# Decays' exponentials on ScalarE, tables spread two per transfer, and query and key products right behind a norm group's turns

## The chip, the cores and the metric

The kernel runs on one core of a Trainium2 chip. The metric is the device time in microseconds (us), the median of the runs.

## What is computed

The reference is a two-layer tower over 16 sequences of 129 tokens with 512 features. A tokenizer makes the tokens; then come a gated-scan layer, a mixture of experts, gated linear attention (GLA), and a second mixture of experts, each with a layer norm ahead and a residual. The change touches the tokenizer and the first pass of the attention.

```python
# tokenizer: 128 heads, 64 states, 512 positions, 16 batches
P = dt_Lambda[..., None] * t - P_max[..., None]
S = jnp.exp(P)                                     # complex
Wc = Wc * num * recip
K = jnp.einsum('chn,hnl->chl', Wc, S).real
...
# attention
q = x @ Wq.T
k_sig = jax.nn.sigmoid(x @ Wk.T)
q = jax.nn.silu(q) * SCALE
gf = jax.nn.log_sigmoid(-k_sig)
o = _gla(q, k_sig, x, gf)
go = o @ Wog.T + x @ Wig.T
```

## The kernel before, in words

**Programs and queues.** Each engine (SyncE for DMAs, VectorE, GpSimd, ScalarE, TensorE) runs one program, written out in order: tokenizer, scan layer, experts, attention, experts. There is no planner. An engine does its instructions in program order, and semaphores hold it where it needs another's result.

**Tokenizer.** Position l is split as 64a + 8b + c, with a, b and c from 0 to 7, so exp(P) is a product of three small tables (`NG` = 3 groups of `TB` = 8 values). The 128 partitions hold 64 states for heads 0 to 63 (`LO`) and the same states for heads 64 to 127 (`HI`). VectorE computes the step sizes, the decay exponents `ke` (L251, 128x1536), the sine and cosine arguments (`im`, `re`), multiplies them by the exponentials (L304), negates one (`ni2`, L306), then forms the coefficients and from them `car`, `ncai`, `ncar` (L338 to L344). ScalarE takes the exponential of `ke` (L392) and the sines (L395, L396). `tab` holds six tables for all 128 heads on both halves; SyncE fills it by SBUF-to-SBUF DMAs of 64 KB (`spread`, L163): for each of four blocks of 32 heads eight for the decay tables (`tables`) and four for the factors (`factors`), 48 in all. The first block's `tables` go when `tabr` is 1, its `factors` when `tabr` is 2, that is behind L344.

The main loop has eight chunks of 16 heads. ScalarE copies the chunk's factors to PSUM (L405), VectorE builds U in two halves (L355, L362, L363), GpSimd builds B (L384, L386, L388), TensorE multiplies them (L429, one product for each head, each in two passes in the trace's count, so x32 is a chunk), ScalarE copies the product out (L416), and SyncE stores it to DRAM (L185) and loads it back with heads on partitions (L192, L215). The scan layer's norm (L482) starts when the last load has landed.

**Attention's first pass.** There are 17 token tiles; the class-token tile (16 rows) goes first, i = 0, and tile n has i = n + 1. VectorE norms them in groups i = 0, 1 to 4, 5 to 10 and 11 to 16 (L482, L506, Newton steps L516 to L522, then one L527 for each tile). TensorE turns each normed tile by four transposes (`turn_tile`, L538) into one of three PSUM banks, ScalarE copies it out (L1946), and TensorE multiplies four copied tiles at a time by the query and key weights (`project`, L2027, eight passes of 512 columns). ScalarE takes query and key out of each product (`band_of`, L1958 and L1959). In TensorE's order `project(-1)`, of the class tokens, stands behind turn 3, `project(0)` behind turn 6, `project(1)` behind turn 10, `project(2)` behind turn 14, and `project(3)` behind turn 16. In ScalarE's order `band_of(0)`, (1) and (2) stand behind the copies of turns 7, 11 and 15, `band_of(3)` at the end. Turn i waits until the copy of turn i-3 is done; `project(q)` waits for the copy of turn 4q+4. Behind the bands come two sigmoids over all sequences (L1974, L1975), a scan and a reciprocal on VectorE (L1816, L1818), and the second pass on TensorE (`xw_of` and `gate_x`, L2055), which begins with turns of its own.

Of the kernel before, what the change touches and what calls it, by code (L numbers as in the profile page):

```python
# [11 lines left out]
ALU = mybir.AluOpType  # L12
# [90 lines left out]
def tokenizer(nc, sem, sb, ps, d, h0, hb, h_in, t_in, stored):  # L103
# [21 lines left out]
    m, kl, ke, mk, re, im = (a.take(NG, HH, TB) for _ in range(6))  # L125
    ni2, car, ncar, ncai, ta, tb = (a.take(HH, TB) for _ in range(6))
    tab = a.take(6, NH, TB)
    R1, I1, D1, D2, A1, A2 = range(6)
# [30 lines left out]
    def sync(sp):  # L159
        def spread(to, half, src, frm, k, s):  # L160

            cols = slice(2 * HC * (k % 2), 2 * HC * (k % 2) + 2 * HC)
            sp.dma_start(tab[half, to, 2 * HC * k:2 * HC * (k + 1), :], src[frm, cols, :]).then_inc(s, 16)  # L163

        def tables(k):
            frm = LO if k < 2 else HI
            for to, lo, hi in ((R1, re[:, 0], re[:, 0]), (D1, re[:, 1], im[:, 1]), (I1, im[:, 0], im[:, 0]), (D2, ni2, re[:, 1])):
                spread(to, LO, lo, frm, k, t_in[k])
                spread(to, HI, hi, frm, k, t_in[k])

        def factors(k):
            frm = LO if k < 2 else HI
            for to, lo, hi in ((A1, car, ncai), (A2, ncai, ncar)):
                spread(to, LO, lo, frm, k, t_in[k])
                spread(to, HI, hi, frm, k, t_in[k])
# [21 lines left out]
        sp.wait_ge(t_in[0], 8 * 16)  # L197
        factors(0)
        for k in range(1, 3):
            tables(k)  # L200
            factors(k)
# [15 lines left out]
    def vector(v):  # L217
# [27 lines left out]
        c.link(v.scalar_tensor_tensor(out=ktf, in0=kc[:, 1, 0:NK], scalar=pos[:, 0:1], in1=kc[:, 0, 0:NK], op0=ALU.mult, op1=ALU.add))  # L245
# [5 lines left out]
        v.tensor_tensor(ke, k24, along(dre), ALU.mult).then_inc(ker, 1)  # L251

# [29 lines left out]

        c.put(v.tensor_tensor(m, k24, along(fhi), ALU.mult))
# [58 lines left out]
        c.put(v.tensor_tensor(car, ta, tb, ALU.subtract))  # L342
        c.link(v.scalar_tensor_tensor(out=ncai, in0=ncai, scalar=-1.0, in1=ncar, op0=ALU.mult, op1=ALU.subtract))
        v.tensor_tensor(ncar, tb, ta, ALU.subtract).then_inc(tabr, 1)  # L344
        v.wait_ge(w_in, 64)
# [19 lines left out]
    def gpsimd(g):  # L365
        for k in range(NHC):
            u = k % 2
            hh = slice(k * HC, (k + 1) * HC)
            if u == 0:
                if k == 0:  # L370
                    g.wait_ge(tabr, 2)
                g.wait_ge(t_in[k // 2], 12 * 16 if k else 8 * 16)
# [17 lines left out]
    def scalar(s):  # L390
        s.wait_ge(ker, 1)
        s.activation(ke, ke, ACT.Exp).then_inc(sines, 1)  # L392
# [5 lines left out]
        def factors(k):  # L398

            if k % 2 == 0:  # L400
                s.wait_ge(t_in[k // 2], 12 * 16)
# [1941 lines left out]
```

## Time and profile before

| | |
|---|---|
| median of 3 runs | 1573.73 us (1570.84 to 1576.62) |
| profiled execution | 1577.39 us, its span 1575.6 us |
| mean granted TensorE clock | 0.968 of full speed |

```profile
PE 1390.4 (88%) x6461; PEld 1080.0 (69%) x6462; DVE 838.1 (53%) x1729; ACT 373.3 (24%) x711; POOL 480.1 (30%) x350
```

This line gives busy time, share of the span and instructions of each engine: PE is TensorE's matmuls, PEld its weight loads, DVE VectorE, ACT ScalarE, POOL GpSimd; SPq is SyncE's queue of DMAs. A tile is named by its tensor: `sb` is the tokenizer's working memory, `ps` PSUM, `moe_xn` the normed tiles, `moe_scratch` holds the turned tiles, `tokens` and `h_rows` are DRAM. The chain that ended last is followed back from the last instruction of the program; its lengths run from one step to the next. In the busy lists, "x8" is a run of eight instructions, and the bracket tells the idle time ahead of it and what ended it.

### The profile page before, as it was taken

Reading aid. Unit: us, or ns where it says so; the run is one execution under the profiler, and the core shown is the slowest. Engines: PE = TensorE matmul, PEld = TensorE weight load, DVE = VectorE, ACT = ScalarE, POOL = GpSimd, SP = SyncE. Lnnn points to the kernel's source line nnn. Section 1 sums busy time; section 2 is a strip of 40 time slices with the busy share of each in tenths; the row PEclk is TensorE's granted clock in tenths of the full one; section 3 lists DMA queues with packets and bytes.
Section 4 is the critical chain, followed back from the end, with each engine's and each line's share of the span. In section 5 each row is a group of like instructions: output and inputs, shape, how many; then the busy total and the mean of one; then the engine's idle time right before and its main releaser. Section 6 shows DMA issues by size and latency. Waiting matters only on the chain.

```text
span 1575.6 us, 21975 instructions
## 1 busy us (share of the span) xinstructions
PE 1390.4 (88%) x6461; PEld 1080.0 (69%) x6462; DVE 838.1 (53%) x1729; ACT 373.3 (24%) x711; POOL 480.1 (30%) x350
## 2 busy tenths in 40 slices
PE   0595648999999999379999889999999999999997
PEld 0583316888544444237777578888888889999896
DVE  8875597755322222563667775555555543333332
ACT  1113113111111111242222312232333212222221
POOL 0661430252244443100111015632332203343332
PEclk9999779999999999798999999999999999999999
DMA  4493005201865554700000403656666579776443
GB/s 97 89 161 39 0 21 179 104 21 63 304 149 93 87 89 72 204 22 0 1 0 1 182 21 97 206 199 212 208 221 225 189 267 361 243 198 185 78 73 41
DMA packets 88931, 197.16 MB, mean 125 GB/s; under 512 B 28657, under 2 KB 32753, under 8 KB 85361
## 3 DMA queue, kind: packets, MB, share of 16 engines
q1 hardware_dynamic: 68768, 154.33, 30.1%
q0 software_dynamic: 20096, 42.02, 14.6%
q8 instruction: 33, 0.54, 0.1%
q14 instruction: 34, 0.27, 0.1%
HBM read 112.24 MB, written 81.02 MB: 123 GB/s over the span
## 4 chain that ended last, share of the span: by engine, by line
PE 79%; DVE 13%; issue 3%; DMA 2%; ACT 1%; POOLq 1%; POOL 0%; SPq 0%; DVEq 0%; ACTq 0%
PE ps L1533 25%; PE ps L1593 19%; PE ps L1655 9%; PE ps L2055 6%; PE ps L1681 4%; PE ps L429 4%; PE ps L1623 2%; DVE held L482 2%; PE ps L538 2%; PE ps L1669 1%; PE ps L778 1%; PE ps L2080 1%; PE ps L779 1%; PE ps L2027 1%; PE ps L2111 1%
## 5 line engine op out<-in xcount | busy, mean ns | idle before, releaser
L1593 PE MATMUL ps<-moe_rounded 128*128 128x384 f32 (+2 forms) x1800 | 374.7, 350 | 0.0
L1593 PEld LDWEIGHTS ps<-moe_rounded 128*128 128x128 f32 x1800 | 326.3, 188 | 33.3
L1300 DVE SCALAR_TENSOR_TENSOR held<-ps,moe_scratch,held 128x512 f32<-128x512 f32 (+1 forms) x255 | 187.5, 747 | 180.8 <-PE ps L1533 180.0
L1533 PE MATMUL ps<-moe_expert_parts,moe_rows_parts 128*128 (+1 forms) x1320 | 258.4, 349 | 2.5 <-DVE moe_rows_parts L1324 1.5
L1533 PE MATMUL ps<-moe_rounded 128*128 128x512 f32 (+3 forms) x885 | 242.2, 394 | 11.8 <-DVE moe_rounded L1282 9.7
L1533 PEld LDWEIGHTS ps<-moe_expert_parts,moe_rows_parts 128*128 128x128 f32 (+1 forms) x1320 | 219.6, 190 | 15.8 <-issue 3.3
L1533 PEld LDWEIGHTS ps<-moe_rounded 128*128 128x128 f32 (+2 forms) x885 | 146.7, 171 | 50.7 <-DVE moe_rounded L1282 12.0
L1310 DVE TENSOR_TENSOR moe_scratch<-moe_scratch,ps 128x256 f32<-128x256 f32 (+1 forms) x80 | 37.7, 471 | 237.2 <-ACT moe_scratch L1515 237.2
L1655 PE MATMUL ps<-moe_experts,moe_scratch 128*128 x320 | 144.2, 593 | 0.6 <-issue 0.6
L1404 POOL TENSOR_TENSOR moe_split_parts<-moe_scratch,moe_split_parts 128x704 fp32r<-128x704 f32 (+2 forms) x48 | 88.6, 1851 | 172.9 <-ACT moe_split_parts L1497 172.9
L1388 POOL DMA_INDIRECT slot_tokens<-moe_scratch x68 | 73.5, 1081 | 174.2 <-DVE held L1300 167.4
L1515 ACT ACTIVATE moe_scratch<-ps 128x256 f32<-128x256 f32 (+1 forms) x80 | 33.9, 424 | 333.5 <-PE ps L1655 193.0
L1484 ACT ACTIVATE moe_scratch<-ps 128x384 f32<-128x384 f32 (+2 forms) x75 | 38.7, 515 | 306.9 <-PE ps L1593 301.5
L429 PE MATMUL ps<-sb 128*128 128x64 f32 x256 | 56.5, 422 | 58.6 <-DVE sb L363 58.3
L2055 PE MATMUL ps<-gla_rounded 128*128 128x512 f32 (+1 forms) x408 | 100.2, 402 | 3.3 <-ACT gla_rounded L1981 2.1
L1655 PEld LDWEIGHTS ps<-moe_experts,moe_scratch 128*128 128x128 f32 x320 | 57.7, 190 | 58.7 <-issue 58.7
L429 PEld LDWEIGHTS ps<-sb 128*128 128x128 f32 x256 | 55.2, 332 | 59.3 <-POOL sb L384 57.9
L538 PE MATMUL ps<-held,moe_xn 128*128 128x128 f32 (+1 forms) x272 | 41.9, 301 | 57.9 <-DVE moe_xn L527 51.1
L2055 PEld LDWEIGHTS ps<-gla_rounded 128*128 128x128 f32 (+1 forms) x408 | 74.7, 186 | 22.6 <-ACT gla_rounded L1981 2.3
L1929 POOL TENSOR_TENSOR moe_xn<-moe_scratch 128x512 f32<-128x512 f32 (+1 forms) x17 | 25.6, 1504 | 201.4 <-DVE moe_scratch L1863 201.4
L538 PEld LDWEIGHTS ps<-held,moe_xn 128*128 128x128 f32 (+1 forms) x272 | 35.3, 158 | 73.2 <-DVE moe_xn L527 36.4
L1681 PE MATMUL ps<-moe_experts,moe_scratch 128*128 x160 | 75.4, 593 | 1.1 <-DVE moe_scratch L1332 1.1
(311 smaller groups left out, 1686.2 us busy)
## 6 DMA issues: line engine op xcount, KB each, us to landing
moe_expert_parts<-expert_parts SPq DMA_DIRECT2D x8, 3840.0 KB, 13.0
expert_parts<-moe_split_parts SPq DMA_DIRECT2D x32, 704.0 KB
moe_scratch<-in_ffn_gate_up SPq DMA_DIRECT2D x32, 352.0 KB, 4.7
xn_rows<-moe_xn SPq DMA_DIRECT2D x2, 4096.0 KB, 12.9
moe_experts<-in_ffn_gate_up SPq DMA_DIRECT2D x8, 1024.0 KB, 6.3
expert_parts<-moe_split_parts SPq DMA_DIRECT2D x8, 1024.0 KB
moe_scratch<-in_ffn_sh_gate_up SPq DMA_DIRECT2D x15, 512.0 KB, 3.5
tokens<-sb SPq DMA_DIRECT2D x16, 256.0 KB
```

Source lines behind the costliest of these rows:

```text
L429: mm = t.matmul(o, ub[:, u, hh, :], bb[:, u, hh, :], start=True, stop=True)
L538: ins = t_eng.transpose(ps_bank[:, k * r:(k + 1) * r], xn[0:r, t, k * P:(k + 1) * P], ident[0:r, 0:r])
L1300: v.scalar_tensor_tensor(out=hb[0:rows, t, :], in0=ps[0:rows, ADDED[t % 3], :], scalar=sg[0:rows, t:t + 1], in1=hb[0:rows, t, :], op0=ALU. ...
L1310: v.tensor_tensor(ehid[:, u], esil[:, u], e_up(u), ALU.mult).then_inc(ehr, 1)
L1388: p.indirect_dma_start(out=slots, out_offset=bass.IndirectOffsetOnAxis(ap=pos_u[0:r, j, t:t + 1], axis=0), in_=tab_u[0:r, t, j, :], in_off ...
L1404: p.tensor_tensor(part[0:rows, x, 1, 0:w], raw[0:rows, x, 0:w], part[0:rows, x, 0, 0:w], ALU.subtract).then_inc(plr, 1)
L1484: s.activation(unit_sil(u, m), unit_banks(u, m)[0], ACT.Silu).then_inc(silr, 1)
L1533: mm = t.matmul(out, lhs(k, x), rhs(k, y), start=(k == 0 and i == 0), stop=(k == ks - 1 and i == 2))
L1593: mm = t.matmul(unit_banks(u, m)[j], weights(k, x, j), xT[y][:, k, unit_cols(m)], start=(k == 0 and i == 0), stop=(k == KD - 1 and i == 2))
L1655: mm = t.matmul(ps[:, u, 0:2 * F], xgT[:, u, k], exg(e, k, 0, 2 * F), start=(k == 0), stop=(k == KD - 1))
L1681: mm = t.matmul(ps[:, 6 + u, :], ehT[0:FR[f], u, f, :], exd(e, f, FR[f]), start=(f == 0), stop=(f == NF - 1))
L2055: mm = t.matmul(out[0:r], xT[:, j % 2, x, k, 0:r], w[:, y, k, :], start=(k == 0 and i == 0), stop=(stop and k == KD - 1 and i == 2))
```

## The change

In the tokenizer, `ke` is no longer multiplied out on VectorE: ScalarE computes exp(scale * dre) in 24 activations of 128x64, one for each of 3x8 table values, the scale being a column of `kt`. The arrays are laid side by side (`powers`, `coeffs`), so that one DMA fills two tables: four for `tables` and two for `factors` in each block, and in block 0 one for `factors`, 23 in all. The LO half of the factors of chunks 0 and 1 is copied by ScalarE from `coeffs` itself and not from `tab`. `car` moves behind `ncar` and raises `tabr` to 3; block 0's factor DMA goes at 2, and GpSimd's first chunk, ScalarE's first factors and the later blocks' DMAs wait for 3. In the attention, `project(0)` moves from behind turn 6 to right behind turn 4, `project(2)` from behind turn 14 to behind turn 16, ahead of `project(3)`; `band_of(0)` and `band_of(1)` move one copy later (behind 8 and 12), `band_of(2)` behind the last copy.

```diff
--- before.py
+++ after.py
@@ -122,10 +122,13 @@
     ri, w2, x2, y2, cc = a.take(2, 2, HH), a.take(2, HH), a.take(2, HH), a.take(2, HH), a.take(2, HH)
     cr, ci = cc[:, 0], cc[:, 1]
     inv, quarter = a.take(HH), a.take(1)
-    m, kl, ke, mk, re, im = (a.take(NG, HH, TB) for _ in range(6))
-    ni2, car, ncar, ncai, ta, tb = (a.take(HH, TB) for _ in range(6))
+    m, kl, ke, mk = (a.take(NG, HH, TB) for _ in range(4))
+    powers, coeffs = a.take(3, NG, HH, TB), a.take(3, HH, TB)
+    im, re = powers[:, 0], powers[:, 1]
+    ta, ni2, tb = (powers[:, 2, g] for g in range(NG))
+    car, ncai, ncar = (coeffs[:, n] for n in range(3))
     tab = a.take(6, NH, TB)
-    R1, I1, D1, D2, A1, A2 = range(6)
+    I1, R1, D1, D2, A1, A2 = range(6)
     ub, bb, bt = a.take(2, HC, TI * NB), a.take(2, HC, TJ), a.take(HC, TJ)
     ob = a.take(2, HC * TJ)
     assert a.at <= TOK_WORDS
@@ -157,22 +160,22 @@
                 sp.dma_start(w[half, :, :].rearrange("p h c -> p (h c)"), d["x"][k]).then_inc(w_in, 16)
     def sync(sp):
-        def spread(to, half, src, frm, k, s):
-
+        def spread(pair, half, src, k):
+            frm = LO if k < 2 else HI
             cols = slice(2 * HC * (k % 2), 2 * HC * (k % 2) + 2 * HC)
-            sp.dma_start(tab[half, to, 2 * HC * k:2 * HC * (k + 1), :], src[frm, cols, :]).then_inc(s, 16)
+            sp.dma_start(tab[half, pair:pair + 2, 2 * HC * k:2 * HC * (k + 1), :], src[frm, :, cols, :]).then_inc(t_in[k], 16)
         def tables(k):
-            frm = LO if k < 2 else HI
-            for to, lo, hi in ((R1, re[:, 0], re[:, 0]), (D1, re[:, 1], im[:, 1]), (I1, im[:, 0], im[:, 0]), (D2, ni2, re[:, 1])):
-                spread(to, LO, lo, frm, k, t_in[k])
-                spread(to, HI, hi, frm, k, t_in[k])
+            spread(I1, LO, powers[:, 0:2, 0], k)
+            spread(I1, HI, powers[:, 0:2, 0], k)
+            spread(D1, LO, powers[:, 1:3, 1], k)
+            spread(D1, HI, powers[:, 0:2, 1], k)
         def factors(k):
-            frm = LO if k < 2 else HI
-            for to, lo, hi in ((A1, car, ncai), (A2, ncai, ncar)):
-                spread(to, LO, lo, frm, k, t_in[k])
-                spread(to, HI, hi, frm, k, t_in[k])
+            if k:
+                spread(A1, LO, coeffs[:, 0:2], k)
+            spread(A1, HI, coeffs[:, 1:3], k)
         h0v = h0.rearrange("h (c i) j -> (c i) h j", i=TI)
@@ -194,8 +197,9 @@
         sp.wait_ge(tabr, 1)
         tables(0)
         sp.wait_ge(tabr, 2)
-        sp.wait_ge(t_in[0], 8 * 16)
+        sp.wait_ge(t_in[0], 4 * 16)
         factors(0)
+        sp.wait_ge(tabr, 3)
         for k in range(1, 3):
             tables(k)
             factors(k)
@@ -242,14 +246,13 @@
         c.link(v.tensor_scalar(pos, lam[:, 0:1], 0.0, None, ALU.is_gt))
         c.put(v.tensor_scalar(sig, pos, -2.0, 1.0, ALU.mult, ALU.add))
         ktf = kt.rearrange("p g k -> p (g k)")
-        c.link(v.scalar_tensor_tensor(out=ktf, in0=kc[:, 1, 0:NK], scalar=pos[:, 0:1], in1=kc[:, 0, 0:NK], op0=ALU.mult, op1=ALU.add))
+        v.scalar_tensor_tensor(out=ktf, in0=kc[:, 1, 0:NK], scalar=pos[:, 0:1], in1=kc[:, 0, 0:NK], op0=ALU.mult, op1=ALU.add).then_inc(ker, 1)
         k24 = bc(kt.unsqueeze(2), 2, HH)
         def along(x):
             return bc(bc(x.unsqueeze(1), 1, NG).unsqueeze(3), 3, TB)
-        v.tensor_tensor(ke, k24, along(dre), ALU.mult).then_inc(ker, 1)
-
+        c.wait()
         c.link(v.tensor_scalar(fa.bitcast(U32), dim.bitcast(U32), 0xFFFFF000, None, ALU.bitwise_and))
         c.put(v.tensor_tensor(fb, dim, fa, ALU.subtract))
         c.link(v.tensor_scalar(p1, fa, V1, None, ALU.mult))
@@ -280,6 +283,7 @@
         def spread(x, w):
             return bc(x.unsqueeze(2), 2, w)
+        v.wait_ge(ker, 1)
         c.put(v.tensor_tensor(m, k24, along(fhi), ALU.mult))
         c.link(v.tensor_tensor(kl, k24, along(flo), ALU.mult))
         c.link(v.tensor_tensor(mk, m, kl, ALU.add))
@@ -339,9 +343,9 @@
         c.put(v.tensor_tensor(tb, CI, AI, ALU.mult))
         c.put(v.tensor_tensor(ncai, CI, AR, ALU.mult))
         c.link(v.tensor_tensor(ncar, CR, AI, ALU.mult))
-        c.put(v.tensor_tensor(car, ta, tb, ALU.subtract))
         c.link(v.scalar_tensor_tensor(out=ncai, in0=ncai, scalar=-1.0, in1=ncar, op0=ALU.mult, op1=ALU.subtract))
         v.tensor_tensor(ncar, tb, ta, ALU.subtract).then_inc(tabr, 1)
+        v.tensor_tensor(car, ta, tb, ALU.subtract).then_inc(tabr, 1)
         v.wait_ge(w_in, 64)
         for k in range(NHC):
@@ -368,8 +372,8 @@
             hh = slice(k * HC, (k + 1) * HC)
             if u == 0:
                 if k == 0:
-                    g.wait_ge(tabr, 2)
-                g.wait_ge(t_in[k // 2], 12 * 16 if k else 8 * 16)
+                    g.wait_ge(tabr, 3)
+                g.wait_ge(t_in[k // 2], 6 * 16 if k else 4 * 16)
             if k >= 2:
                 g.wait_ge(prod, 2 * (k - 1))
             B4 = bb[:, u].rearrange("p h (b c) -> p h b c", c=TB)
@@ -389,7 +393,10 @@
     def scalar(s):
         s.wait_ge(ker, 1)
-        s.activation(ke, ke, ACT.Exp).then_inc(sines, 1)
+        for g in range(NG):
+            for k in range(TB):
+                ins = s.activation(ke[:, g, :, k], dre, ACT.Exp, scale=kt[:, g, k:k + 1])
+        ins.then_inc(sines, 1)
         for n, (sine, cosine) in enumerate(((im, re), (sm[4], sm[3]))):
             s.wait_ge(arg, n + 1)
             s.activation(sine, sine, ACT.Sin, scale=-TWO_PI).then_inc(sines, 1)
@@ -397,12 +404,18 @@
         def factors(k):
+            hh = slice(k * HC, (k + 1) * HC)
+            to = ps[:, 6 + k % 2, 0:2 * HC * TI].rearrange("p (t h i) -> p t h i", t=2, i=TI)
+            if k < 2:
+                s.wait_ge(tabr, 3)
+                s.activation(to[LO], coeffs[LO, 0:2, hh], ACT.Copy)
+                s.wait_ge(t_in[0], 5 * 16)
+                s.activation(to[HI], tab[HI, A1:A2 + 1, hh, :], ACT.Copy).then_inc(apr, 1)
+                return
             if k % 2 == 0:
-                s.wait_ge(t_in[k // 2], 12 * 16)
-            if k >= 2:
-                s.wait_ge(ur, 2 * (k - 1))
-            hh = slice(k * HC, (k + 1) * HC)
-            s.activation(ps[:, 6 + k % 2, 0:2 * HC * TI].rearrange("p (t h i) -> p t h i", t=2, i=TI), tab[:, A1:A2 + 1, hh, :], ACT.Copy).then_inc(apr, 1)
+                s.wait_ge(t_in[k // 2], 6 * 16)
+            s.wait_ge(ur, 2 * (k - 1))
+            s.activation(to, tab[:, A1:A2 + 1, hh, :], ACT.Copy).then_inc(apr, 1)
         factors(0)
         for k in range(NHC):
@@ -1966,9 +1979,11 @@
                     if to is not None:
                         s.wait_ge(c3, 2)
                         s.activation(to, xn[0:NB, NB, :], ACT.Copy).then_inc(c3, 1)
-            if i % 4 == 3 and i > 4:
-                band_of((i - 7) // 4)
-        for q in range(NG - 1, NG):
+            if i == 8:
+                band_of(0)
+            if i == 12:
+                band_of(1)
+        for q in range(2, NG):
             band_of(q)
         s.wait_ge(bnd, 4 * NG)
         s.activation(sq, qr, ACT.Sigmoid).then_inc(bnd, 1)
@@ -2034,9 +2049,12 @@
             turn_tile(t, ps[:, TB1[i % 3], :], xn, n, ident).then_inc(turned, 1)
             if i == 3:
                 project(-1)
-            if i % 4 == 2 and i > 4:
-                project((i - 6) // 4)
-        project(NG - 1)
+            if i == 4:
+                project(0)
+            if i == 10:
+                project(1)
+        for q in range(2, NG):
+            project(q)
         PARTS = ((0, 0), (0, 1), (1, 0))
@@ -2141,7 +2159,7 @@
 EXPERTS = NE * (KD * 2 * 352 + 3 * D)
 RING = 4
 DEEP = 4
-TOK_LOADED, TOK_STORED = (12 * 16,) * 3, (12 * 16, NHC * 16, NHC * 16)
+TOK_LOADED, TOK_STORED = (5 * 16, 6 * 16, 6 * 16), (6 * 16, NHC * 16, NHC * 16)
 PARTS = RING * 2 * (KD * 2 * 352 + 3 * D)
 SPLIT = 3 * 2 * 2 * D
 ROWS = 2 * 2 * (KD + 3) * P
```

## Rows read from the trace of the kernel before

**Rows 1.** Page, the chain that ended last, by line: share of the span.
```profile
PE ps L1533 25%; PE ps L1593 19%; PE ps L1655 9%; PE ps L2055 6%; PE ps L1681 4%; PE ps L429 4%; PE ps L1623 2%; DVE held L482 2%; PE ps L538 2%; PE ps L1669 1%; PE ps L778 1%; PE ps L2080 1%; PE ps L779 1%; PE ps L2027 1%; PE ps L2111 1%
```

**Rows 2.** Stage: length, busy us (count) of PE, PEld, DVE, ACT, POOL, clock, DMA.
```profile
58.00:115.00 57.00, 56.41 (x256) 55.20 (x256) 51.67 (x39) 10.63 (x21) 41.01 (x20) 1.00 0.92 157
```

**Rows 3.** Chain that ended last, tokenizer: start us, length us, what.
```profile
8.88 1.76 DVE sb L251
...
47.75 0.61 DVE sb L343
...
49.11 0.46 SPq L163
...
50.89 2.05 DMA sb<-sb
...
53.45 2.29 DVE sb L355
...
58.29 7.06 PE ps L429 x32
...
120.87 5.68 DMA held<-tokens
```

**Rows 4.** Timeline of the tokenizer: start us, us, engine, line, operation [idle before].
```profile
10.68 1.48 ACT L392 ACTIVATE sb<-sb 128x1536 f32<-128x1536 f32 x1 [8.64 <-DVE sb L251]
...
27.32 1.48 ACT L395 ACTIVATE sb<-sb 128x1536 f32<-128x1536 f32 x1 [13.86 <-DVE sb L288]
...
49.17 1.94 POOL L384 TENSOR_TENSOR sb<-sb 128x1024 f32<-128x1024 f32 x1 [48.07 <-DVE sb L344]
...
53.09 2.35 POOL L388 TENSOR_TENSOR sb<-sb 128x1024 f32<-128x1024 f32 x1
```

**Rows 5.** ScalarE's groups by shape, 657 to 700 us: count | busy us, mean ns.
```profile
L1946 ACT ACTIVATE moe_scratch<-ps 128x512 f32<-128x512 f32 x16 | 9.1, 597 | 19.9 <-PE ps L538 19.8
...
L1942 ACT ACTIVATE sb<-ps 128x64 f32<-128x64 f32 x1 | 0.2, 224 | 1.0 <-PE ps L538 1.0
```

**Rows 6.** DMA issues: count, KB each, median us from issue to landing.
```profile
sb<-sb SPq DMA_DIRECT2D x48, 64.0 KB, 2.0
...
gla_raw<-in_Wqk SPq DMA_DIRECT2D x1, 128.0 KB, 3.9
```

**Rows 7.** Timeline of the attention's first pass.
```profile
670.94 0.60 ACT L1946 ACTIVATE moe_scratch<-ps 128x512 f32<-128x512 f32 x1
...
671.60 1.97 PE L538 MATMUL ps<-held,moe_xn 128*128 128x128 f32 x8 [4.22 <-DVE moe_xn L527]
...
673.50 5.25 PE L2027 MATMUL ps<-moe_scratch,gla_raw 128*64 128x512 f32 x8
...
680.40 2.83 DVE L527 TENSOR_SCALAR moe_xn<-held 128x512 f32<-128x512 f32 x6
...
686.62 0.59 ACT L1958 ACTIVATE sb<-ps 32x512 f32<-32x512 f32 x1
...
687.84 1.57 ACT L1946 ACTIVATE moe_scratch<-ps 128x512 f32<-128x512 f32 x3
688.49 0.19 PEld L2027 LDWEIGHTS ps<-moe_scratch,gla_raw 128*64 128x64 f32 x2 [1.36 <-ACT moe_scratch L1946]
...
692.76 0.60 ACT L1946 ACTIVATE moe_scratch<-ps 128x512 f32<-128x512 f32 x1 [3.35 <-PE ps L538]
...
695.25 3.65 PE L2027 MATMUL ps<-moe_scratch,gla_raw 128*64 128x512 f32 x8 [2.09 <-ACT moe_scratch L1946]
```

**Rows 8.** Chain that ended last, attention: start us, length us, what.
```profile
681.73 3.65 PE ps L2027 x8
...
708.83 5.73 PE ps L2055 x24
```

**Rows 9.** TensorE in short stretches: length, busy us (count), granted clock, DMA.
```profile
676.00:677.00 1.00, 1.00 (x3) 0.62 0.00 0
...
718.00:720.00 2.00, 2.00 (x6) 0.50 0.00 0
```

## The prediction

> **What bounds the kernel now.** I read the chain that ended last first, by line. The experts' products (L1533, L1593, L1655, L1681) hold most of it, all on TensorE, and the change leaves them alone; the lines that it touches, L429 and L2027, hold 4% and 1% [rows 1]. So the change can shorten only two stretches, and the question is what ends last in each. Everything behind them starts from their results and should move forward as it stands: the norm behind the tokenizer waits for the last load from DRAM [rows 3], and the attention's second pass for the query and key bands.
>
> *Tokenizer.* The chain of the first 58 us runs through VectorE alone (L251 is one link of it), then through SyncE: L344 ends at 49.09, four factor DMAs go out from 49.11, the last at 50.89, and that one takes 2.05 us to land; ScalarE's copy follows, and VectorE starts U at 53.45 [rows 3]. TensorE's first product starts at 58.29, and from there a chunk takes 7.06 us; between 58 and 115 us TensorE is busy for 56.41 of 57 us at full clock [rows 2, 3]. So the main loop has no gaps to lose, and only its start can move.
>
> *Attention.* TensorE does `project(0)` from 673.50, (1) from 681.73, (2) from 688.49 and (3) from 695.25 [rows 7, 8]. The first takes 5.25 us, the others 3.65. The normed tiles are there long before: the last six are written by 683.23 [rows 7], while the copy of a turn among them still starts at 692.76. What holds it is the ring of TensorE and ScalarE: (2) and (3) each begin when a copy of ScalarE's ends (the bracket names L1946), and the bands stand between those copies [rows 7].
>
> **The change part by part: tokenizer.**
>
> 1. *The exponentials' product leaves VectorE.* L251 goes, -1.76 us [rows 3]. The next instruction waits only for what ran ahead of L251, so nothing takes its place. In return ScalarE does 24 activations of 128x64. A 128x64 copy took 0.224 us, a 128x512 one 0.597 [rows 5], so the 24 cost between 5.4 and 14.3 us, and I take 6, near the row of the same width. From about 8.9 us they end at 14.9 (at worst at 23.2), and the table load for the sines (1.28 us) still ends before the sine arguments come, at 27.32 - 1.76 = 25.56 [rows 4]. Hidden at both ends. If the cover were gone, each microsecond past 24.3 would count in full, since both sines and L304 are on the chain. The Trainium skill ("ScalarE: Activation LUTs", "What ACT_TABLE_LOAD costs") gives an activation with immediate scale 186 ns plus 0.833 ns for each element of width, about 93 ns more for a per-partition scale, and 93 ns of overlap back to back; estimated from that page the 24 take 24 x 0.24 = 5.8 us, which changes no term.
>
> 2. *`car` moves behind `ncar`.* One 128x512 step, 0.61 us [rows 3], leaves the way to the factor DMA, -0.61. It is behind it now, and holds GpSimd's start (below).
>
> 3. *One factor DMA instead of four.* The last of the four went out at 50.89, the first at 49.11 [rows 3]: -1.78. The one that remains carries 128 KB where the rows had 64. The 48 of 64 KB landed in 2.0 us, one load of 128 KB from DRAM in 3.9 [rows 6]. I take 2.2, near the row with the same two ends in SBUF, so +0.15, and +1.85 as the other bound; a gain is excluded, since twice the data on the same queue can't land sooner. ScalarE's copy becomes two, LO and HI. LO waits for `car` at about 47.3 and is over by 47.7, before the DMA lands at about 48.9, and HI alone follows; one copy stood there before too. Nothing.
>
> Sum for VectorE's U: -1.76 - 0.61 - 1.78 + 0.15 = -4.0, so it starts at 49.45.
>
> 4. *GpSimd's B.* It starts behind L344 now, at 49.17, and ends at 55.44 [rows 4]. In the changed kernel it waits for `car`, which ends when `ncar` ended before, less 1.76: B is ready at 55.44 - 1.76 = 53.7. U's first half is ready at 58.29 - 4.0 = 54.3, so TensorE still waits for VectorE. This caps the part at 58.29 - 53.7 = 4.6 however fast the DMA is.
>
> 5. *The other DMAs.* SyncE issues 23 instead of 48. The stores behind them come earlier, but the end of the tokenizer is TensorE's last chunk, one store and one load of 5.68 us [rows 3], which keep their lengths: nothing. Chunks 2 and later need their tables later than before relative to landing. The extra wait of SyncE for `tabr` 3 holds only the later blocks, six DMAs that go out about 1.8 us earlier than before.
>
> Tokenizer: -4.0 (bounds -4.6, by GpSimd, and -2.3, by the 3.9 us landing).
>
> **The change part by part: attention.**
>
> 6. *`project(0)` behind turn 4.* It waits for the copy of turn 4, which ends at 671.54 [rows 7], behind the class tokens' bands and copies. TensorE is idle until 671.60 anyway, so it starts there, 1.9 us before now, and turns 5 and 6 go behind it. Now those eight passes take 5.25 us and not 3.65 because the clock rises from 1.2 to 2.4 GHz at about 676.7 (0.62 over that microsecond) [rows 7, 9]. If it rises at the same moment, six passes at 0.86 and two at 0.43 end at 677.6. At 1.2 GHz throughout it would end at 678.5. Then turns 5 to 8: the first copy starts 0.62 behind the product (688.49 + 3.65 to 692.76 [rows 7]), each copy takes 0.62 with its gap, so the copy of turn 8 ends 3.1 us later and `project(1)` starts at 680.7 instead of 681.73: -1.0 (bounds -0.1 and, with the clock up at the first pass's end, -3).
>
> The Trainium skill ("TensorE: Matmul & The Clock Gate", "Part 1: The HAM clock gate") says that the array is throttled by default and that activity releases it. That speaks against this edit: it puts the widest products at the head of a burst, where they run cold. By the rule the whole of `project(0)` might be at 1.2 GHz; the 678.5 above is that case.
>
> 7. *`project(2)` behind turn 16.* From the end of `project(1)`, now: 13.5 us to the end of (3) (685.38 to 698.90) [rows 7, 8]. In the changed kernel: 0.62 to the copy of turn 11, two copies 1.24, `band_of(1)` 1.22 (686.62 to 687.84 [rows 7]), the copy of turn 13, 0.62, turn 16 on TensorE 0.55 (half of one of the two turns that took 1.97 us at 1.2 GHz [rows 7], and its start), then (2) and (3) back to back, 7.3: 11.6 us. -1.9. The normed tiles are ready, since turn 11's is written by 681. ScalarE copies turn 16 under `project(2)`, takes band 2 under `project(3)`, and the end is the same: band 3, two sigmoids. Bounds: if the copies kept TensorE for one place more, 0.6 is lost, -1.3; if turn 16 needn't wait, 0.6 is won.
>
> Attention: -2.9 (bounds -1.4 and -5.5).
>
> **Sum** against the profiled execution's own time: 1577.4 - 4.0 - 2.9 = 1570.5. That execution was 3.7 us over the median of the runs, and the runs differ by 5.8 us among themselves; the saving is the same for the median: 1573.7 - 6.9 = **1566.8 us**.
>
> **Rivals.**
>
> *A slow pair transfer (R1).* Landing 3.9 instead of 2.2: -2.3 in the tokenizer, -5.2 in all, 1568.5. For it speaks only a row from DRAM; against it the median of 2.0 over 48 transfers.
>
> *Cold project(0) (R2).* All eight passes at 1.2 GHz, -0.1 instead of -1.0: -6.0, 1567.7. TensorE is idle 4.22 us ahead of it [rows 7].
>
> *The clock falls in the longer light stretch (R3).* Between (1) and (2) TensorE has only turns and waits for ScalarE for 4.3 us, where the stretches between products now are 3.1 (685.38 to 688.49, and 688.49 + 3.65 to 695.25). After light work ahead of 718 the clock stood at 0.50 there [rows 9], and came back near 727.3, some 9.4 us. The same behind 684 costs half of it, 4.7: -2.2 in all, 1571.5. Against it: six transposes in 4.3 us are not idle, and now the clock holds through both stretches of 3.1.
>
> *Slower: the clock falls there and stays low into the second pass (R4).* If (2) and (3) run at 1.2 GHz (16 passes at 0.86 for 0.455, +6.5) and the 24 passes from 708.83, 5.73 us at full clock [rows 8], do too (+5.7), that is +12.2 - 6.9 = +5.3, 1579.0. It decides once more than 6.9 us of chained full-clock work is done at half, that is over 13.8 us of low clock under products where the profile's low stretch lasted 9.4; the idle time between bands and second pass would have to keep it down.
>
> *The attention part does nothing (R5).* If the end of the first pass were set by VectorE's norms, moving products would give nothing: -4.0, 1569.7. Against it is the last tile, written by 683.23, while a turn is still copied at 692.76 [rows 7].
>
> **How the numbers follow.** Forecast 0.56; R1 0.10, R2 0.10, R3 0.12, R4 0.04, R5 0.08. A measurement of this kernel can tell about 0.3%, 4.7 us, from no change. The forecast, R2 and R1 lie beyond that, R1 barely; R3 and R5 lie within; R4 is slower. Medians move by 1.5 us either way with the clock's luck, so a part of the nearer cases changes sides: faster 0.74, same 0.22, slower 0.04. The range takes the bounds of the sum (-4.6 - 5.5 = -10.1 and -2.3 - 1.4 = -3.7, each with both parts at its end, so seldom met) with 1.5 to 2 us for the clock's luck: 1561.5 to 1572, which lets in R3 and leaves out R4 and the tails.
>
> **What would show it.** In the changed profile: 24 activations at L396's place between 9 and 16 us and no 1.76 us step at 8.9; VectorE's U at 49.4 and TensorE's first product at 54.3, released by VectorE (by GpSimd, if the cap of step 4 binds); the pair transfer's landing at 2.2; TensorE's last tokenizer chunk ending 4.0 earlier, the norm starting at 122.6. In the attention, relative to the norm's first step: `project(0)` 18.1 us behind it, and from its start to the end of `project(3)` 24.4 us (671.6 to 696.0 on the old scale; now 673.5 to 698.9). A TensorE clock under 1.0 between (1) and (3) would show R3. The prediction is wrong if either stretch keeps its length, or if a later stretch gives the time back.

## The result, and the profile after

The changed kernel takes 1568.38 us (median of 14 runs, 1565.49 to 1571.15), the kernel before 1575.27 (median of 14, 1570.84 to 1577.83). The ratio is 0.996, with a 95% interval from 0.995 to 0.997, so 6.9 us or 0.44% are saved. The profiled execution took 1569.5 us, its span is 1567.7 where it was 1575.6.

The head of the page and the chain that ended last, by line:

```profile
span 1567.7 us, 21991 instructions
PE ps L1546 25%; PE ps L1606 19%; PE ps L1668 9%; PE ps L2073 6%; PE ps L1694 4%; PE ps L442 4%; PE ps L1636 2%; PE ps L551 2%; DVE held L495 2%; PE ps L1682 1%; PE ps L791 1%; PE ps L2042 1%; PE ps L792 1%; PE ps L2098 1%; DVE held L1313 1%
```

The lines have moved by 13 and more, the shares have not: the experts still hold the chain (L1546 was L1533), L442 is the tokenizer's product (was L429), L2042 the query and key product (was L2027). The two stretches must be looked at one by one.

*Tokenizer*, chain that ended last (start us, length us, what), against [rows 3]:

```profile
45.99 0.69 DVE sb L347
46.71 2.36 DMA sb<-sb
49.09 0.39 ACT ps L413
49.58 2.29 DVE sb L359
...
54.41 7.06 PE ps L442 x32
...
111.84 5.09 DMA tokens<-sb
116.95 5.63 DMA held<-tokens
122.67 2.48 DVE held L495 x4
```

One transfer stands between `ncar` (L347) and ScalarE's copy, where SyncE issued four. U starts at 49.58 instead of 53.45, the first product at 54.41 instead of 58.29, a chunk still takes 7.06 us, and the last load ends 4.0 us earlier. Timeline of ScalarE and GpSimd, against [rows 4]:

```profile
8.87 5.90 ACT L398 ACTIVATE sb<-sb 128x64 f32<-128x64 f32 x24 [6.83 <-DVE sb L249]
14.78 1.28 ACT L402 ACT_TABLE_LOAD   x1
25.50 1.48 ACT L402 ACTIVATE sb<-sb 128x1536 f32<-128x1536 f32 x1 [9.44 <-DVE sb L292]
47.37 1.94 POOL L388 TENSOR_TENSOR sb<-sb 128x1024 f32<-128x1024 f32 x1 [46.28 <-DVE sb L348]
```

The 24 exponentials end at 14.8 and the sines still wait 9.4 us for VectorE.

*Attention's first pass*, timeline (start us, us, engine, line), against [rows 7, 8]:

```profile
651.01 0.68 DVE L495 BATCH_NORM_STATS2 held<-held 16x6 f32<-16x512 f32 x1 [10.37 <-DMA held<-h_rows]
669.21 5.59 PE L2042 MATMUL ps<-moe_scratch,gla_raw 128*64 128x512 f32 x8 [3.76 <-ACT moe_scratch L1959]
674.73 3.05 PE L551 MATMUL ps<-held,moe_xn 128*128 128x128 f32 x24
675.43 2.07 ACT L1959 ACTIVATE moe_scratch<-ps 128x512 f32<-128x512 f32 x4 [6.27 <-PE ps L551]
677.71 3.65 PE L2042 MATMUL ps<-moe_scratch,gla_raw 128*64 128x512 f32 x8
685.05 0.63 PE L551 MATMUL ps<-held,moe_xn 128*128 128x128 f32 x4 [1.22 <-ACT moe_scratch L1959]
685.61 7.08 PE L2042 MATMUL ps<-moe_scratch,gla_raw 128*64 128x512 f32 x16
```

I count from the first norm statistics of this layer (651.01; before 653.51). `project(0)` starts at 18.2 where it started at 20.0, `project(1)` ends at 30.3 instead of 31.9, and (2) and (3) run as one piece of 7.08 us that ends at 41.7 instead of 45.4. The wait of 1.22 ahead of 685.05 is turn 16, held by ScalarE's copies. "Statistics" below means this first instruction.

Between the two stretches, 1.2 us are lost. GpSimd's last store of token rows starts 3.7 us earlier than before, at 638.36 instead of 642.08, but the attention's statistics only 2.5. Chain of the changed kernel:

```profile
638.36 9.82 DMA h_rows<-held,moe_scratch
648.39 2.60 DMA held<-h_rows
```

The same two took 8.93 and 2.28 us in the kernel before.

### The profile page after: what moved, and what is told of

The parts are those of the page before. It is cut to its first block, busy times and chain, and to the rows that moved or that the text cites. A ratio compares the mean times of both kernels' runs of the same rounds, so it can differ in the third digit from the quotient of the medians.

```text
span 1567.7 us, 21991 instructions
## 1 busy us (share of the span) xinstructions
PE 1390.0 (89%) x6461; PEld 1079.8 (69%) x6462; DVE 836.6 (53%) x1728; ACT 378.3 (24%) x736; POOL 480.3 (31%) x350
## 3 DMA queue, kind: packets, MB, share of 16 engines
q1 hardware_dynamic: 68240, 154.20, 30.4%
## 4 chain that ended last, share of the span: by engine, by line
PE 79%; DVE 12%; issue 3%; DMA 2%; ACT 2%; POOLq 1%; POOL 0%; DVEq 0%; ACTq 0%; SPq 0%
PE ps L1546 25%; PE ps L1606 19%; PE ps L1668 9%; PE ps L2073 6%; PE ps L1694 4%; PE ps L442 4%; PE ps L1636 2%; PE ps L551 2%; DVE held L495 2%; PE ps L1682 1%; PE ps L791 1%; PE ps L2042 1%; PE ps L792 1%; PE ps L2098 1%; DVE held L1313 1%
## 5 line engine op out<-in xcount | busy, mean ns | idle before, releaser
L1546 PE MATMUL ps<-moe_expert_parts,moe_rows_parts 128*128 (+1 forms) x1320 | 258.2, 348 | 2.6 <-DVE moe_rows_parts L1337 1.5
L1546 PE MATMUL ps<-moe_rounded 128*128 128x512 f32 (+3 forms) x885 | 242.3, 394 | 11.8 <-DVE moe_rounded L1295 9.8
L1546 PEld LDWEIGHTS ps<-moe_expert_parts,moe_rows_parts 128*128 128x128 f32 (+1 forms) x1320 | 219.5, 190 | 15.7 <-issue 3.3
L1546 PEld LDWEIGHTS ps<-moe_rounded 128*128 128x128 f32 (+2 forms) x885 | 146.8, 171 | 50.7 <-DVE moe_rounded L1295 12.0
L442 PE MATMUL ps<-sb 128*128 128x64 f32 x256 | 56.5, 422 | 54.7 <-DVE sb L367 54.4
L442 PEld LDWEIGHTS ps<-sb 128*128 128x128 f32 x256 | 55.2, 332 | 55.4 <-POOL sb L392 54.0
L551 PEld LDWEIGHTS ps<-held,moe_xn 128*128 128x128 f32 (+1 forms) x272 | 34.6, 156 | 70.0 <-issue 34.4
```

Of the source, the lines that this page charges most:

```text
L442: mm = t.matmul(o, ub[:, u, hh, :], bb[:, u, hh, :], start=True, stop=True)
L551: ins = t_eng.transpose(ps_bank[:, k * r:(k + 1) * r], xn[0:r, t, k * P:(k + 1) * P], ident[0:r, 0:r])
L1546: mm = t.matmul(out, lhs(k, x), rhs(k, y), start=(k == 0 and i == 0), stop=(k == ks - 1 and i == 2))
```

## The experiments

Each label names one kernel. Times in the tables are from the profiled execution. "First product" is the first product of the tokenizer; the attention is counted from its first norm statistics, as above. Six kernels without a ratio below ran once: exp_x4 took 1571.4 us, no_factor_dma 1565.8, factor_two 1567.5, p0_only 1570.2, band1_last 1567.5 and cls_after4 1567.0. Executions of one kernel lie up to 7 us apart, so these times settle nothing, and only the profiles are used.

| kernel | U starts | first product | `project(1)` ends | `project(3)` ends | last row store to statistics |
|---|---|---|---|---|---|
| before | 53.45 | 58.29 | 31.9 | 45.4 | 11.4 |
| changed | 49.58 | 54.41 | 30.3 | 41.7 | 12.7 |
| tok_only | 49.53 | 54.35 | 31.8 | 45.3 | 11.4 |
| att_only | 53.39 | 58.22 | 30.3 | 41.7 | 11.6 |
| exp_only | 51.64 | 56.47 | 32.0 | 45.5 | 11.3 |
| exp_x4 | 55.81 | 60.63 | 30.4 | 41.7 | 11.7 |
| no_factor_dma | 48.16 | 53.66 | 30.2 | 41.6 | 12.3 |
| factor_two | 49.68 | 54.51 | 30.0 | 41.4 | 12.5 |
| p0_only | 49.46 | 54.29 | 30.3 | 43.9 | 11.4 |
| band1_last | 49.65 | 54.48 | 29.9 | 39.9 | 12.4 |
| cls_after4 | 49.54 | 54.37 | 27.1 | 38.9 | 11.8 |
| all3 | 48.14 | 53.65 | 26.8 | 37.6 | 12.4 |

**One part alone.** My theory: the parts are independent and add up. Rival: one of them is given back later.

tok_only takes the tokenizer of the changed kernel and the attention of before.

> The changed tokenizer with the attention of before. If the two parts add up as in the prediction's sum, the time is 4.0 us under before (ratio 0.9975), the profile shows the first product of the tokenizer at 54.4 us instead of 58.3, and the attention's first pass keeps its 45.4 us from the first norm statistics to the end of project(3). Rival: the tokenizer's gain is given back at the store of token rows ahead of the attention (changed kernel: 638.36 to 651.01 where before had 642.08 to 653.51); then the time is 2.5 to 2.8 us under before.

Measured: 1572.58 us against 1575.67, ratio 0.9984 (0.9975 to 0.9993), that is 1.1 to 3.9 us saved. The first product stands where it stands in the changed kernel, and the attention's first pass is the one of before.

att_only takes the attention of the changed kernel and the tokenizer of before.

> The attention of the changed kernel with the tokenizer of before. By the sum of the prediction the time is 2.9 us under before; by the changed kernel's profile, where the first pass took 41.7 us instead of 45.4, it is 3.7 us under. The first product of the tokenizer stays at 58.3 us. Rival: the part gives nothing (VectorE's norms or the clock decide), then the first pass takes 45.4 us again or the second pass is longer by what the first won.

Measured: 1572.88 us against 1575.67, ratio 0.9982 (0.9973 to 0.9991), 1.4 to 4.2 us saved. The first pass ends at 41.7, as in the changed kernel. The profiles of the two show both stretches moved by the full amount, each without the other:

```profile
54.35 18.04 PE L442 MATMUL ps<-sb 128*128 128x64 f32 x81 [54.35 <-DVE sb L367]
```
```profile
689.83 7.08 PE L2029 MATMUL ps<-moe_scratch,gla_raw 128*64 128x512 f32 x16
```

The first line is of tok_only, the second of att_only. The times, 2.5 and 2.8 us by the ratios, are smaller than the stretches' 3.9 and 3.7; the upper end of tok_only's interval is just the 3.9, and att_only's interval holds the 3.7. The stages between the stretches vary between executions by about as much: from the first statistics of the scan layer to the last row store they took from 514.5 to 517.3 us in the twelve kernels of the table, though nothing in them differs. In tok_only's profile the last store of the tokenizer took 5.74 us where it took 5.09 in the changed kernel. So the profiles show each stretch moved whole and by itself, and the times agree with that at the edge of their intervals, no better. (By its profile att_only gained another 0.8 us in the second pass, told below; 4.5 us lies just outside its interval.) For tok_only the time is as near to the rival as to the theory: 2.5 us is what the rival gave. Its place is not borne out, since tok_only took 11.4 us at the row store, as before.

**The exponentials alone, and their cover.** exp_only is the kernel before with this edit:

```diff
-        v.tensor_tensor(ke, k24, along(dre), ALU.mult).then_inc(ker, 1)
+        c.wait()
...
-        s.activation(ke, ke, ACT.Exp).then_inc(sines, 1)
+        for g in range(NG):
+            for k in range(TB):
+                ins = s.activation(ke[:, g, :, k], dre, ACT.Exp, scale=kt[:, g, k:k + 1])
+        ins.then_inc(sines, 1)
```

> Kernel before with one edit: the decays' exponentials are 24 activations with a scale for each table value, and VectorE's product of 128x1536 is gone. Prediction: 1.76 us under before, first product of the tokenizer at 56.5 us. Rival: the 24 activations end too late for the sines, then the start of the sines (25.5 us here) waits for ScalarE and the gain is smaller.

Measured: first product at 56.47, 1.82 earlier than before; 1572.6 us against 1575.67, ratio 0.9991 (0.9981 to 1.0001). The step is in the profile; the time agrees with it and can't tell it from nothing.

exp_x4 asks what happens when ScalarE is late. It runs the loop three times more, into unused memory, ahead of the one that counts.

> Changed kernel with 72 more activations of 128x64 into unused memory ahead of the 24 that count, so that ScalarE's work ahead of the sines is 4 x 5.9 = 23.6 us and ends at 32.5 us, its table load at 33.8. Prediction's step 1: each microsecond past 24.3 us counts in full, so the first product comes 8.2 us later, at 62.6 us. Rival: VectorE has 3.1 us of its own work (arguments of the second pair of sines) between the first sine arguments and the product that needs the sines, so only 33.8 + 1.5 + 1.5 + 1.7 = 38.4 against 32.0 us counts: 6.4 us later, at 60.8 us. Third: nothing moves, if the sines don't bound.

```profile
8.90 17.29 ACT L399 ACTIVATE sb<-sb 128x64 f32<-128x64 f32 x72 [6.87 <-DVE sb L249]
26.09 5.88 ACT L402 ACTIVATE sb<-sb 128x64 f32<-128x64 f32 x24
31.99 1.28 ACT L406 ACT_TABLE_LOAD   x1
33.28 1.48 ACT L406 ACTIVATE sb<-sb 128x1536 f32<-128x1536 f32 x1
...
34.80 3.43 DVE L308 TENSOR_TENSOR sb<-sb 128x1536 f32<-128x1536 f32 x2 [6.13 <-ACT sb L406]
```

The exponentials now end at 32.0 and VectorE's product with the sines (L308) waits 6.13 us for them. The first product comes at 60.63, 6.2 us later: near the rival's 6.4, not the 8.2 of the prediction's step 1. VectorE's own 3.1 us between the first sine arguments and L308 cover a part of any delay. In the changed kernel the table load ends at 16.1, L308 starts at 28.56, and the first sine takes 1.48, so ScalarE could be late by 11 us (28.56 - 1.48 - 16.1) before anything moved.

**The factors.** The prediction put 1.6 us on "one DMA instead of four". factor_two splits the one that is left into two of 64 KB:

```diff
-            spread(A1, HI, coeffs[:, 1:3], k)
+            if k:
+                spread(A1, HI, coeffs[:, 1:3], k)
+            else:
+                for n in range(2):
+                    sp.dma_start(tab[HI, A1 + n, 0:2 * HC, :], coeffs[LO, 1 + n, 0:2 * HC, :]).then_inc(t_in[0], 16)
```

> Changed kernel with block 0's factor DMA split again into two of 64 KB. Theory that the issue pitch of SyncE (0.64 us) is what pairing saves, and the larger transfer costs 0.3 to 0.4 us of landing (2.36 in the changed kernel, 2.05 before): the second lands 0.64 + 2.05 = 2.7 us behind the first issue, so VectorE's U starts 0.3 us later, at 49.9 us, first product at 54.7. Rival: pairing gains the whole 0.64 us, U at 50.2.

```profile
46.61 0.48 SPq L182
...
47.14 2.03 DMA sb<-sb
```

U starts at 49.68, 0.10 later than in the changed kernel, but here `ncar` was ready 0.1 us sooner (the first transfer goes out at 46.61, there at 46.71), so the way from there to U is 0.2 longer. The second transfer goes out 0.53 us behind the first and lands in 2.03; the pair lands in 2.36. Pairing saves a pitch of 0.53 and pays 0.33 of it back in landing, which is the same 0.2. From the first factor DMA to U the kernel before took 4.34 us (49.11 to 53.45), the changed kernel 2.87. Of these 1.5 us, 1.3 come from the two LO transfers that ScalarE's copy from `coeffs` makes needless, and 0.2 from pairing.

no_factor_dma takes the wait for the last transfer away too (it is still issued):

```diff
-                s.wait_ge(t_in[0], 5 * 16)
-                s.activation(to[HI], tab[HI, A1:A2 + 1, hh, :], ACT.Copy).then_inc(apr, 1)
+                s.activation(to[HI], coeffs[LO, 1:3, hh], ACT.Copy).then_inc(apr, 1)
```

> Changed kernel in which ScalarE's HI copy of the first two chunks' factors reads the coefficients of the LO half and waits for no DMA, so the output of heads 0 to 31 is wrong in part. VectorE's U could then start at 48.2 us instead of 49.6, and its first half be ready at 53.0. Prediction's step 4 (GpSimd as the cap, B ready at 53.65 us): the first product starts at 53.7 us, released by GpSimd, 0.7 us earlier than the 54.4 of the changed kernel and not 1.4. Rival, no cap: first product at 53.0 us.

The expectation is mistaken on one thing: nothing is wrong in the output. Block 0's factor DMA spreads just these rows, `coeffs` 1 and 2 of the LO half, to the HI half, and ScalarE's copy does the same on its way to PSUM. Chain of this kernel:

```profile
46.64 0.61 DVE sb L348
...
47.33 1.94 POOL sb L388
49.27 1.92 POOL sb L390
...
51.26 2.36 POOL sb L392
...
53.66 8.37 PE ps L441 x38
```

U starts 1.4 us earlier, at 48.16, the first product 0.75, at 53.66, and the chain now goes through GpSimd's three steps. This is the cap of the prediction's step 4.

**The two moved projects.** p0_only keeps `project(0)` and band 0 where the change has them and puts the others back:

```diff
-        for q in range(2, NG):
-            project(q)
+            if i == 14:
+                project(2)
+        project(NG - 1)
```

> Changed kernel with project(2) and the bands 1 and 2 back in the places of before; only project(0) and band 0 are moved. Prediction: project(0) starts 18.2 us behind the first norm statistics instead of 20.0, and project(1) ends 1.0 us earlier relative to those statistics than before (30.9 us instead of 31.9; the changed kernel had 30.3), project(3) 44.4 instead of 45.4. Rival: the gain of project(0) is given back before project(3), then it ends at 45.4.

`project(1)` ends at 30.3 and `project(3)` at 43.9, 0.6 and 0.5 us earlier than expected. Of the 3.7 us, 1.5 come from `project(0)`, and 2.2 from `project(2)` behind turn 16, and neither is given back before the end.

band1_last and cls_after4 ask what holds the ring. The first takes band 1 behind the last copy, the second the class tokens' bands behind the copy of turn 4:

```diff
-            if i == 12:
-                band_of(1)
-        for q in range(2, NG):
+        for q in range(1, NG):
```
```diff
-            if i == 3:
+            if i == 4:
                 band_cls()
```

> Changed kernel with band 1 behind the last copy instead of behind the copy of turn 12. Theory that the ring of copies sets the start of turn 16 and with it project(2): project(2) starts 33.4 us behind the first norm statistics instead of 34.6, project(3) ends at 40.5 instead of 41.7. Rival: TensorE or VectorE bounds, nothing moves.

> Changed kernel with the class tokens' bands (with their table load, some 4.4 us of ScalarE) behind the copy of turn 4 instead of ahead of it. Theory that this copy sets project(0): it starts 14.8 us behind the first norm statistics instead of 18.2, project(1) ends by 25.4, and then VectorE's normed tiles are late: turn 11 starts at 27.5 instead of 30.4, project(3) ends at 38.8 instead of 41.7. Rival: project(0) moves, but ends with the others as before, because turns 5 to 10 wait for VectorE; then project(3) ends at 41.7.

Products of band1_last, then of cls_after4, whose statistics start at 650.61 and 652.17:

```profile
683.46 7.08 PE L2040 MATMUL ps<-moe_scratch,gla_raw 128*64 128x512 f32 x16
```
```profile
667.29 5.38 PE L2042 MATMUL ps<-moe_scratch,gla_raw 128*64 128x512 f32 x8 [0.69 <-ACT moe_scratch L1959]
675.58 3.65 PE L2042 MATMUL ps<-moe_scratch,gla_raw 128*64 128x512 f32 x8
684.01 7.08 PE L2042 MATMUL ps<-moe_scratch,gla_raw 128*64 128x512 f32 x16
```

Both theories hold. With band 1 out of the way the pair of products starts at 32.85 instead of 34.6 and ends 1.8 us earlier, of which 0.4 is a shorter `project(0)` (5.19 instead of 5.59: TensorE's clock rose 3.1 us into it and not 3.9). With the class bands out of the way `project(0)` starts at 15.1. `project(1)` then ends at 27.1 and not by 25.4 as expected, since `project(0)` ends at 20.5 and turns 5 to 8 with their copies take 2.9 us behind it. The end at 38.9 is the expected 38.8: turn 11 starts at 27.5, when VectorE has written the first tile of its last norm group, and from there the ring runs as in the changed kernel.

**All three together, and what GpSimd's wait is for.** all3 is the changed kernel with the edits of no_factor_dma (the factor DMA of block 0 is dropped with it), band1_last and cls_after4.

> Changed kernel with three further edits: block 0's factor DMA is gone (ScalarE copies the HI factors of the first two chunks from the LO half's coefficients), band 1 is taken behind the last copy, and the class tokens' bands behind the copy of turn 4. Expected from the profiles: first product at 53.7 us (-0.75 against the changed kernel), project(3) ends 37.6 us behind the first norm statistics instead of 41.7 (-4.1), in all -4.8 against the changed kernel, about 1563.5 us and -11.7 against before. Rival: VectorE's norms bound the first pass sooner than worked out, or the second pass takes back what the first wins; then under 2 us are left.

Measured: 1561.74 us against 1575.60, ratio 0.9914 (0.9900 to 0.9929). That is 13.6 us under before by the ratio (11.2 to 15.8), where 11.7 was expected, and it is faster than both kernels. Its first product starts at 53.65 and its first pass ends at 37.6, both as expected. Its first pass:

```profile
663.76 5.09 PE L2039 MATMUL ps<-moe_scratch,gla_raw 128*64 128x512 f32 x8 [0.69 <-ACT moe_scratch L1958]
...
676.14 3.04 PE L550 MATMUL ps<-held,moe_xn 128*128 128x128 f32 x24 [0.73 <-DVE moe_xn L539]
679.11 7.08 PE L2039 MATMUL ps<-moe_scratch,gla_raw 128*64 128x512 f32 x16
```

The bracket at 676.14 names L539, VectorE's normed tile. Behind it the turns and the pair of products follow without a wait, so the ring is no longer what ends last.

b_early goes one step further and drops GpSimd's wait for `tabr` 3, since its first chunk needs only the decay tables:

```diff
-                if k == 0:
-                    g.wait_ge(tabr, 3)
```

> Kernel with the three edits of the first run of this job, and GpSimd's first chunk no longer held for the coefficients (it needs only the decay tables, landed by about 38 us). Theory that the wait for tabr keeps GpSimd off VectorE's time for nothing: the first product starts with VectorE at 53.0 us. Rival, the two engines slow each other: VectorE's steps between 38 and 47 us grow, and the first product comes at 53.7 us or later.

```profile
36.82 0.23 DVE L236 TENSOR_SCALAR sb<-sb 128x128 int32<-128x128 f32 x1
37.02 1.94 POOL L386 TENSOR_TENSOR sb<-sb 128x1024 f32<-128x1024 f32 x1 [35.92 <-DMA sb<-sb]
37.08 1.96 DVE L237 TENSOR_SCALAR sb<-sb 128x128 int32<-128x128 int32 x1
38.92 1.94 POOL L388 TENSOR_TENSOR sb<-sb 128x1024 f32<-128x1024 f32 x1
39.08 1.94 DVE L315 TENSOR_TENSOR sb<-sb 128x128 f32<-128x128 f32 x1
40.94 2.34 POOL L390 TENSOR_TENSOR sb<-sb 128x1024 f32<-128x1024 f32 x1
41.05 2.38 DVE L316 SCALAR_TENSOR_TENSOR sb<-sb 128x128 f32<-128x128 f32 x1
...
59.23 2.29 DVE L359 TENSOR_TENSOR sb<-sb,ps 128x2048 f32<-128x2048 f32 x1 [0.91 <-ACT ps L410]
...
64.05 8.20 PE L439 MATMUL ps<-sb 128*128 128x64 f32 x36 [64.05 <-DVE sb L367]
```

The rival, and far harder than I thought. VectorE's L237 takes 1.96 us where L236, with the same shape, took 0.23 just before GpSimd began. Each of six VectorE steps lasts about as long as the GpSimd step beside it, and the first product comes at 64.05, 10.4 us later than in all3; the one execution took 1575.06 us. The Trainium skill ("SBUF — State Buffer", "SBUF: two separate sides") says that VectorE and GpSimd share a pair of ports, and that a GpSimd instruction, or one of VectorE's in a two-port mode or with two inputs in SBUF, holds the pair for its whole length while the other is blocked. By that rule this is what should be seen, and the trace agrees. U's step is not hindered: it reads one operand from PSUM, and takes 2.29 us with GpSimd beside it (49.58 in the changed kernel) as without (59.23 here, where GpSimd's last step ended at 49.82).

## Why the prediction was right

The forecast was -6.9 us and the medians gave -6.9. (The forecast time, 1566.8, is 1.6 short, because the median of before is 1575.27 over 14 runs and was 1573.73 over three.) Both stretches moved by the mechanisms that were forecast, but that close a match is luck. By the profiles the tokenizer gave 4.0 us, 0.3 of it went in the scan layer, 1.2 at the row store, and the attention's first pass gave 3.7: 6.2 when the second pass begins. The spans differ by 7.9. Of the other 1.7 us, 0.8 come in the second pass, and the prediction had no term for them. The third of VectorE's steps `moe_scratch<-ps,gla_raw` 128x128 there starts 78.2 to 78.4 us behind the statistics in the three kernels with the attention of before (before, tok_only, exp_only) and 72.1 to 73.8 in the five with the changed attention (changed, att_only, exp_x4, no_factor_dma, factor_two; the changed kernel 73.8), that is 4.4 earlier or more, and not 3.7. With it goes another course of the clock (below, R3 and R4). The last 0.9 us are short waits in the last experts, where nothing was changed, and no run shows that they belong to the change. The steps in order:

- *Step 1, the exponentials.* -1.76 forecast; VectorE's L283 started at 14.69 before and starts as L287 at 12.88, -1.81. The 24 activations took 5.90 us; 6 was taken, and the estimate beside it was 5.8. The row of the same width was the right end to choose. What was wrong is the sentence on the lost cover, as exp_x4 showed: a delay counts less, by VectorE's work between arguments and use.
- *Steps 2 and 3, the way to U.* `car` behind `ncar` gave 0.6: the transfer goes out at 46.71 against 49.11, -2.4, of which 1.8 are step 1. The landing of the pair was 2.36, not 2.2, which is the whole difference between U's 49.58 and the 49.45 forecast. The number was right, the reason half: factor_two shows that pairing as such is worth 0.2 us, and leaving two transfers out 1.3. R1, a landing of 3.9, did not occur.
- *Step 4, the cap by GpSimd.* B was forecast ready at 53.7. no_factor_dma shows it by the first product at 53.66, released by GpSimd. What GpSimd's wait is good for, the prediction doesn't say; b_early shows it.
- *Step 5.* The norm started at 122.67, forecast 122.6. From the first product to it both kernels took 68.3 us, so the paired tables of the later blocks gave and cost nothing there.
- *Step 6, `project(0)`.* It started 18.2 behind the statistics, forecast 18.1, and took 5.59 us with the clock rising under it (0.50 from 668 to 673, 0.96 from 673 to 675), where 6.0 was forecast. The prediction let the clock rise at the same moment as before, 23.2 us behind the statistics; it rose at 22.1. So `project(0)` ended at 23.8 and not 24.1, and with the copies (next point) `project(1)` ended 1.5 us earlier than before, not 1.0. The prediction's 0.43 and 0.86 us for a pass stand in none of its rows. The first is borne out by the pair of products (7.08 - 3.65 = 3.43 for the second eight), and the second is twice it, at half the clock. R2, the whole at 1.2 GHz, 6.9 us by the 0.86, did not occur in any profile: it took from 5.09 to 6.02.
- *Step 7, `project(2)`.* -2.2 instead of -1.9. Two terms of the sums were mis-sized. The pair of products was put at 7.3, twice 3.65, and took 7.08, since passes follow each other without a gap; that is 0.2 of the 0.3. A copy was put at 0.62, but copies that stand back to back overlap, four took 2.07 us; with 0.2 us from the last copy to the product, which the prediction left out, this gave 0.2 us in step 6 and almost nothing in step 7.
- *R3 and R4, the clock.* The clock did not fall in the light stretch between (1) and (3). It fell later, in both kernels, under the second pass. In the changed kernel:

```profile
675.00:680.00 5.00, 5.00 (x30) 1.00 0.00 0
680.00:685.00 5.00, 3.84 (x24) 1.00 0.01 2
685.00:690.00 5.00, 4.95 (x15) 1.00 0.01 3
...
697.00:699.00 2.00, 2.00 (x7) 0.51 0.00 0
...
716.00:718.00 2.00, 2.00 (x6) 0.50 0.00 0
```

  The columns are length, TensorE's busy us, granted clock and DMA. The low stretch from 697 on is not in the profile of before. There TensorE had 1.2 us idle between the second pass's first two blocks of 24 passes (5.72 and 5.73 us); now they run as one piece of 12.73, so the slow clock took up the idle time and cost 0.1 us (12.73 against 12.64 from the start of the one block to the end of the other). The one at 716 answers to the one of [rows 9], but it lasts about 7 us (to 721) where that one lasted about 10 (718 to 727.5), and the two passes of L2111, which took 1.74 us under it, take 1.02 ahead of it. This is the 0.8 us that the second pass gained. att_only's clock ran the same course; in exp_x4 it was low only from 64 to 67 us behind the statistics. Why it runs otherwise behind the shorter first pass, no run tests.
- *R5, the attention part does nothing.* Excluded by att_only. But VectorE's norms were only 2.8 us from being the bound: the first tile of the last group is written 27.5 us behind the statistics (677.92 + 0.56), and turn 11 started at 30.3; in cls_after4 it started at 27.5.

What stays open is the 1.2 us at the row store. The kernels took either 11.3 to 11.8 or 12.3 to 12.7 us there, and what was edited doesn't sort them: exp_x4 and cls_after4 have the whole change and took 11.7 and 11.8, while no_factor_dma, factor_two, band1_last and all3 took the longer, as the changed kernel did. The time at which the last row store starts does sort them, without an exception. The five that start it by 638.36 us took the longer; the other eight, from tok_only's 638.52 on (b_early is one, with 11.3), the shorter. If that is more than chance over one profile of each, the loss is a price of coming early. No run moves the start alone. The rows' store runs beside two weight loads of 1 MB, but SyncE issues them at the same distance from the store in the kernels before, changed and tok_only (the first of its loads 1.0 us ahead of it), so another order of issue is not the reason.

## What to carry to other kernels

Where two engines pass work back and forth through a few buffers, follow the order written on the one that the other waits for, and put what nobody waits for (here the bands) last: the two moved bands ended the first pass 4.1 us earlier still, more than the change itself won there. Before pairing transfers, ask whether each is needed: a copy that runs anyway may read from the source, across partitions. A wait that looks too strict may keep two engines off each other; look at the durations of both while they overlap before removing it.

## What was not expected of the hardware

- Beside a GpSimd step of 1.94 to 2.37 us a VectorE step of 0.23 to 0.38 us took 1.94 to 2.52 us, when all its operands were in SBUF; a step of 2.29 us with an operand in PSUM kept its time.
- An SBUF-to-SBUF transfer of 64 KB landed in 2.0 us, one of 128 KB in 2.36, with a pitch of 0.50 to 0.64 us between issues.
- ScalarE copies from 64 partitions to the other 64 on its way to PSUM in 0.38 us, the time of the copy without the shift.
